# Token rows in order, inverted places and gathers between additions in a routed expert kernel

## What is computed

```python
x = x + _L1_ffn_ref(_layernorm(x), Wr, br, W1, b1, W2, b2)

def _L1_ffn_ref(x, Wr, br, W1, b1, W2, b2):      # E = 8 experts, D = 256, H = 1024
    scores = einsum('bsd,de->bse', x, Wr) + br
    _, topk_idx = top_k(scores, 2)
    indicator = one_hot(topk_idx, E).sum(-2)
    weights = softmax(where(indicator > 0, scores, -inf), axis=-1)
    for i in range(E):
        h = relu(x * indicator[..., i:i+1] @ W1[i] + b1[i])
        out = out + (h @ W2[i] + b2[i]) * weights[..., i:i+1]
    return out
```

## Time and profile before

| | |
|---|---|
| median of 3 runs | 1434.64 us |
| profiled execution, its own time | 1434.98 us |
| its span from first to last instruction | 1433.2 us |
| PE busy, share of the span | 1231.8 us, 86% |
| VectorE busy | 1025.3 us, 72% |
| ScalarE busy | 802.4 us, 56% |
| GpSimd busy | 522.3 us, 36% |
| mean granted clock of TensorE | 0.911 of 2.4 GHz |
| `route` block, about | 896 to 1007 us |
| `experts` block, about | 1007 to 1433 us |

### The profile page before, as it was taken

How to read it: one execution, slowest core, us unless ns; L and a number is a source line. 1 busy time by engine, 2 the same in 40 slices (tenths; PEclk the granted TensorE clock), 3 DMA queues, 4 the chain that set the end, 5 groups by cost and what they waited for, 6 DMA issues and landing times. The chain is left out here.

```text
span 1433.2 us, 28369 instructions
## 1 busy us (share of the span) xinstructions
PE 1231.8 (86%) x8633; PEld 930.1 (65%) x8634; DVE 1025.3 (72%) x2058; ACT 802.4 (56%) x1212; POOL 522.3 (36%) x423
## 2 busy tenths in 40 slices
PE   8959999976999594997999998741799999999995
PEld 4526777763433283784677676741689889998874
DVE  3759999877989686676788988766465665666543
ACT  2545665564679787636788876650333443344341
POOL 2027777720000000001887875576033223232322
PEclk9989999999999656999999999555899999999998
DMA  6020000000024675101132232565223232223210
GB/s 225 1 70 1 1 0 0 0 1 1 0 89 176 236 238 176 72 1 48 37 128 88 88 117 74 172 202 180 68 52 48 44 55 45 46 45 53 47 29 7
DMA packets 61447, 106.06 MB, mean 74 GB/s; under 512 B 7488, under 2 KB 48704, under 8 KB 60736
## 3 DMA queue, kind: packets, MB, share of 16 engines
q1 hardware_dynamic: 48080, 88.24, 19.2%
q0 software_dynamic: 13296, 16.92, 6.3%
HBM read 66.96 MB, written 39.10 MB: 74 GB/s over the span
## 5 line engine op out<-in xcount | busy, mean ns | idle before, releaser
L2308 POOL DMA_INDIRECT out<-ex_yo,ex_mt x71 | 115.4, 1625 | 314.4 <-DVE ex_yo L2283 170.9
L2217 ACT ACTIVATE ex_hT<-ex_ps_h,e_b1T,e_unscale 128x256 f32<-128x256 f32 (+1 forms) x312 | 143.9, 545 | 113.3 <-PE ex_ps_h L2174 113.3
L2174 PE MATMUL ex_ps_h<-ex_xT_hi,a_arena 128*128 128x256 f16 (+1 forms) x1248 | 203.5, 265 | 0.3 <-issue 0.2
L607 PE MATMUL at_ps_y<-c_VW,at_pT_hi 128*128 (+1 forms) x1024 | 171.1, 273 | 3.5 <-DVE main_x_res L740 3.5
L927 POOL TENSOR_TENSOR at_sc<-at_sc,at_ri 128x960 f32<-128x960 f32 (+1 forms) x96 | 145.2, 1527 | 68.7 <-DVE at_ri L735 68.0
L2174 PE MATMUL ex_ps_h<-ex_xT_lo,a_arena 128*128 128x256 f16 (+1 forms) x624 | 164.5, 264 | 0.0
L585 PE MATMUL at_ps_s<-a_arena,at_xnT_hi 128*128 (+1 forms) x512 | 158.8, 393 | 4.3 <-issue 4.3
L2187 PE MATMUL ex_ps_y<-a_arena,ex_hT_hi 128*128 x568 | 154.9, 273 | 4.7 <-DVE ex_hT_lo L2265 4.1
L2187 PE MATMUL ex_ps_y<-e_w_lo,ex_hT_hi 128*128 x568 | 154.9, 273 | 0.0
L2187 PE MATMUL ex_ps_y<-a_arena,ex_hT_lo 128*128 x568 | 154.8, 273 | 0.0
L927 POOL TENSOR_TENSOR at_sc<-at_sc,at_mx 128x960 f32<-128x960 f32 (+1 forms) x96 | 134.1, 1411 | 26.0 <-DVE at_mx L712 25.9
(11 more groups left out here) (350 smaller groups left out, 2811.0 us busy)
## 6 DMA issues: line engine op xcount, KB each, us to landing
at_half<-in_L_ffn_W SPq DMA_DIRECT2D x32, 512.0 KB, 4.0
up_scratch<-gm_stg SPq DMA_DIRECT2D x16, 768.0 KB, 3.2
gm_stg<-up_scratch SPq DMA_DIRECT2D x16, 768.0 KB, 4.3
ex_row<-xs SPq DMA_DIRECT2D x32, 260.0 KB, 3.0
rt_stage<-in_L_ffn_W SPq DMA_DIRECT2D x16, 512.0 KB, 5.4
main_x_res<-in_x SPq DMA_DIRECT2D x8, 512.0 KB, 12.1
out<-main_x_res SPq DMA_DIRECT2D x8, 512.0 KB, 6.3
xs<-rt_pad SPq DMA_DIRECT2D x18, 130.0 KB, 2.4
```

Of the source, the lines that this page charges most:

```text
L607: last = nc.tensor.matmul(ps_y[:, 0:D], a[j][:, n, :], b[:, bass.ds(off + n * D, D)], start=(n == 0 and i == 0), stop=(n == NP - 1 and i = ...
L2174: last = nc.tensor.matmul(ps_h[:, n, at], a[:, bass.ds(e * WN + d * HID + n * P, P)], b[:, d, at], start=(m == 0), stop=(m == 3 * DT - 1))
L2217: last = nc.scalar.activation(hT[:, n, at], ps_h[:, n, at], ACT.Relu, bias=b1T[:, bass.ds(e * HT + n, 1)], scale=unscale[:, 0, bass.ds(e, 1)])
L2308: nc.gpsimd.indirect_dma_start(out=acc[:, :], out_offset=bass.IndirectOffsetOnAxis(ap=mt[j][:, q, 1:2].bitcast(U32), axis=0), in_=yo[j][:, ...
```

## The change

In `route`, a token's row is sent once, in token order, by SP (one store for a group of four tiles). Positions are no longer computed per group: the one-hot vectors of all 32 tiles are kept, and after the last group VectorE computes for every token and both experts the place (slot and lane) that the row has in the experts' tiles. These places are inverted on PE: VectorE builds two 0/1 matrices per 16 token tiles and choice, GpSimd and ScalarE multiply one of them by the tile's number and by the lane's number, and 64 products sum them up, so that each lane of each of the 71 slots of 128 rows gets the number of its row in `xs`, in the table `slot`. Five small operations per group go from VectorE to GpSimd. In `experts`, a row tile is fetched by two indirect DMAs on GpSimd's queue, one for each slot, into one of four buffers; SP loads nothing there but a bias. Loops on PE, ScalarE and VectorE are unrolled by four instead of two, and GpSimd's is written out. The core of the diff:

```diff
@@ route, SP @@
-            sp.wait_ge(cnt_r, 1)
-            for e in range(E):
-                n = nc.sync.value_load(cnt[0:1, e:e + 1], min_val=0, max_val=T)
-                for q in range(TR // P):
-                    sp.dma_start(xs[bass.ds(n + (e * CAP + q * P), P), :], pad[:, :]).then_inc(padded, 16)
+            for c in range(NK):
+                sp.wait_ge(xn_r, TK * (c + 1))
+                sp.wait_ge(pay_r, c + 1)
+                sp.dma_start(xs[(TK * c + 1) * P:(TK * (c + 1) + 1) * P, :].rearrange("(i p) d -> p i d", p=P), pay[c % NB][:, :, :]
+                             ).then_inc(sent[c % NB], 16)
+                for q in range(NS + highs_to(c), min(NS + highs_to(c + 1), 2 * E)):
+                    load_half(q)
@@ route, GpSimd @@
-                for k in range(2):
-                    g.indirect_dma_start(out=xs[:, :], out_offset=bass.IndirectOffsetOnAxis(ap=pos[c % NB][:, i, k:k + 1], axis=0),
-                                         in_=pay[c % NB][:, i, :], in_offset=None, bounds_check=last_row,
-                                         oob_is_err=True).then_inc(sent[t % (NB * TK)], 16)
+                g.tensor_tensor(ind[:, mine, :], oh[:, 0, mine, :], oh[:, 1, mine, :], ALU.add).then_inc(ind_r, 1)
...
+            for n in range(NG):
+                pool.wait_ge(spot_r, n + 1)
+                need(pool, slot_mm, n - 1)
+                t0 = GR * n % NT
+                g.tensor_tensor(in_slot[n % 2][:, 0, :, :], is_slot[n % 2],
+                                turn_no[:, t0:t0 + GR].unsqueeze(2).to_broadcast([P, GR, SLOTS]), ALU.mult).then_inc(turn_r, 1)
@@ route, PE @@
+                for i in range(GR):
+                    last = nc.tensor.matmul(ps_i[:, 0:2 * SLOTS], in_lane[:, GR * g + i, :], in_slot[g % 2][:, :, i, :],
+                                            start=(g == 0 and i == 0), stop=(g == NG - 1 and i == GR - 1))
@@ route, VectorE: spread(g), four times @@
+                v.tensor_tensor(is_slot[g % 2], line[:, 0:SLOTS].unsqueeze(1).to_broadcast([P, GR, SLOTS]),
+                                part_f[:, 1, mine].unsqueeze(2).to_broadcast([P, GR, SLOTS]), ALU.is_equal).then_inc(spot_r, 1)
+                v.tensor_tensor(in_lane[:, mine, :], line[:, :].unsqueeze(1).to_broadcast([P, GR, P]),
+                                part_f[:, 0, mine].unsqueeze(2).to_broadcast([P, GR, P]), ALU.is_equal).then_inc(lane_r, 1)
@@ experts, SP @@
-                    sp.dma_start(row[j][:, q0:q1, :], xs[bass.ds(r * rows, rows), :].rearrange("(q p) d -> p q d", p=P)
-                                 ).then_inc(row_in[j], 16)
@@ experts, GpSimd @@
+            def fetch(i, q):
+                need(pool, t_r, i - RB + 1)
+                need(pool, meta_r, i - RB + 1)
+                n = 2 * i + q
+                nc.gpsimd.indirect_dma_start(out=row[i % RB][:, q, :], out_offset=None, in_=xs[:, :],
+                                             in_offset=bass.IndirectOffsetOnAxis(ap=slot[:, n:n + 1].bitcast(U32), axis=0),
+                                             bounds_check=last_sent, oob_is_err=True).then_inc(row_in[i % RB], 16)
+            for i in range(3):
+                for q in range(Q):
+                    fetch(i, q)
+            for k in range(NTL + 1):
+                for q in range(Q):
+                    if k and q < rows_of(k - 1).stop:
+                        add(k - 1, q)
+                    if there(k + 3, NTL) and q < rows_of(k + 3).stop:
+                        fetch(k + 3, q)
```

More of the change, by code:

```diff
@@ L1847, in _ @@
                     score(t - 1)
-                if t % TK == 2 and t > TK:
-                    rank(t // TK - 1)
             score(NT - 1)
-            rank(NK - 1)
+            rank()
+            for g in range(NG):
+                to_slots(g)
         @block.scalar
@@ L1891, in _ @@
             ratio(NK - 1)
+            for g in range(NG):
+                act.wait_ge(spot_r, g + 1)
+                need(act, slot_mm, g - 1)
+                nc.scalar.activation(in_slot[g % 2][:, 1, :, :], is_slot[g % 2], ACT.Copy, scale=lane[:, 0:1]).then_inc(slot_r, 1)
         @block.vector
@@ L1979, in place @@
             def place(c):
[L1981 to L1983 removed]
+                need(dve, pay_r, c)
                 dve.wait_ge(e_r, c + 1)
                 link_on(v.tensor_scalar(wt[:, 0, :], wt[:, 1, :], 1.0, None, ALU.add))
[L1986 to L1988 removed]
@@ L2006, in place @@
-                link_on(last)
-                for n in range(2):
-                    last = v.tensor_reduce(posf[:, :, n], oh[:, n, :, :], AX.X, ALU.add)
-                link_on(last)
-                v.tensor_copy(pos[c % NB][:, :, :], posf[:, :, :]).then_inc(meta_r, 1)
+                v.reciprocal(wt[:, 2, :], wt[:, 0, :]).then_inc(inv_r, 1)
             def lows(a, b):
@@ new lines, in _ @@
+            then(v.tensor_tensor(begin[:, 1, :], begin[:, 1, :], begin[:, 0, :], ALU.subtract))
+            then(v.tensor_tensor(incl[:, :, :], incl[:, :, :], begin[:, 1, :].unsqueeze(1).to_broadcast([P, NT, E]), ALU.mult))
+            then(v.tensor_tensor(after[:, :, :], after[:, :, :], incl[:, :, :], ALU.add))
+            for i in range(2):
+                last = v.tensor_tensor(oh[:, i, :, :], oh[:, i, :, :], after[:, :, :], ALU.mult)
+            then(last)
+            then(v.tensor_reduce(spot[:, :], oh[:, :, :, :].rearrange("p n t e -> p (n t) e"), AX.X, ALU.add))
@@ L2074, in experts @@
+            lows(highs_to(NK - 1), highs_to(NK))
+            dve.wait_ge(slot_mm, NG)
+            then(v.tensor_copy(lane_v[:, :], ps_i[:, SLOTS:2 * SLOTS]))
+            v.scalar_tensor_tensor(out=slot[:, :], in0=ps_i[:, 0:SLOTS], scalar=float(P), in1=lane_v[:, :],
+                                   op0=ALU.mult, op1=ALU.add)
+def experts(nc, b2, b1T, eid, x_res, w1, w2, unscale, ident, xs, acc, table, slot):
     Q = TR // P
     with Scope(nc, "ex") as s:
-        row = [s.sb(f"row{j}", [P, Q, ROW]) for j in range(2)]
+        RB = 4
+        row = [x_res[:, E:, :].rearrange("p t d -> p (t d)")[:, j * Q * ROW:(j + 1) * Q * ROW].rearrange("p (q d) -> p q d", q=Q)
+               for j in range(RB)]
@@ L2179, in down @@
             def down(i, j):
-                spans = [(look_up(nc.tensor, 1, n, E - 1), range(q0, q1)) for n, q0, q1 in runs(i)]
+                spans = [(expert(nc.tensor, n), range(q0, q1)) for n, q0, q1 in runs(i)]
                 pe.wait_ge(hlo_r, 2 * i + 2)
@@ L2210, in relu @@
             def relu(i, j):
[L2211 removed]
+                spans = [(expert(nc.scalar, n), slice(q0 * P, q1 * P)) for n, q0, q1 in runs(i)]
                 for g in range(2):
```

279 lines of the change are left out of this document (143 added, 136 removed).

## The result

The changed kernel takes 1541.22 us (median of 4 runs, 1538.81 to 1544.16), the kernel before 1426.16 us (4 runs, 1415.17 to 1437.44): a ratio of 1.0836, 95% interval 1.0733 to 1.0938. The profiled execution took 1544.16 us, its span 1542.0. By their times two of the four runs of before have this long start (1434.64 and 1437.44 us) and none of the changed kernel's, so the ratio is a little low: against 1417.6 us, the median of the 13 runs of before taken beside e1, it is 1.087.

The account below looks back on a forecast made before the run. PE was taken to bound the expert loop and no engine to be full in routing; 1434.98 + 114 (30 steps, 3.80 us wait each) - 5 (routing) = 1544 us, range 1485 to 1605.

Parts of the forecast that it names:

- The chain of a step: Expert loop: from one step's start through yo, additions and second gather to PE's next start, 14.72 us against 10.92.
- The estimate of 2.3 us: Expert loop: alternative time for a 133 KB gather to land, in place of 3.0; total 21 us lower.
- The mixed steps cover it: Expert loop after the 30 lengthened steps: mixed steps already take 15.12 us, so the 14.72 us chain adds nothing.
- The clock rival: Expert loop: waits let TensorE's clock fall, opening transposition +0.5 us per step, 15 us, 1559 in all; chance 0.13.
- the share of three quarters for PE: Expert loop, a sign: PE's busy share falls to about three quarters, from 50.00 of 50 us.
- The routing: Before the expert loop: 17 us gained in the group loop, 11.8 lost computing places after it, a gain of 5 us.
- the term for `spread`: Routing, after the last one-hot: four times `spread` on VectorE, 14.5 us, with the multiplications and PE's products running under it.
- the 2.1 us per group in the loop: Routing loop: each of 8 groups falls from 8.56 to 6.5 us, 17 us earlier at the last one-hot.
- The 243 GB/s: Routing loop: transfer rate taken to limit each group, 1.58 MB in 6.5 us.
- The low end of the forecast's range: Whole kernel: 1485 us, from a chain of 13.0 us and -12 for the routing.
- First transposition and last one-hot: End of routing, signs: last one-hot near 967 us, first expert transposition near 1005 us.
- The sign that was to show the forecast wrong: End of routing: the prediction is wrong if the first expert transposition is later than 1015 us.

Follow-up runs that it names:

- e1: Changed kernel with both gathers ahead of both additions in each turn of GpSimd's loop: 1422.31 us, ratio to the kernel before 1.0041.
- e4: Changed kernel with eight row buffers instead of four and gathers for tile k+4 instead of k+3, still alternating with the additions: 1424.67 us.
- e5: On top of e1, GpSimd's multiplication under `spread` made by ScalarE, as 16 small operations per group: 1414.08 us.
- e7: On top of e1, the five small routing operations per group moved from GpSimd back to VectorE: 1433.82 us, in an execution with the long start.
- e0: The kernel before, unchanged, run once more with a profile: 1419.83 us.

## Why the prediction came out, step by step

- **The chain of a step: right, term by term.** Forecast 4.88 to the first addition, 5.0, 1.84, 3.0, 14.72; measured 4.78, 4.71, 2.08, 3.30, 14.88. From the last gather's start to PE's, which no row of before had, it was 2.9 us at the median of the 21 steps in which that gather's issue took 1.06 us or little more, and 3.7 on the mean of the nine in which it took 1.8. The loss in 30 steps was 118 us against 114. That the place in the queue is the cause, and not slower transfers, e1 to e4 show. The estimate of 2.3 us from the Trainium skill's page on DMA ("DMA: Bandwidth & Descriptors", "Anatomy of one DMA — SWDGE (gpsimd) path") would have been 0.6 too low against that 2.9, and 1.0 against the mean of 3.30.
- **The mixed steps cover it: nearly.** The rest behind tile 33 grew by 4.6 us where nothing was forecast. The first mixed stretch ran at a granted clock of 0.89, that of e1 at 1.00 (1347.4 to 1361.9), and e1's rest is 74.2 us long.
- **The clock rival: right that it falls, wrong in its price.** With waits of 2 to 4 us ahead of each step the granted clock was 0.93 over the 30 steps, where it was 1.00: in 15 stretches, 58 us in all, it stood at 0.50. But the rival's 0.5 us per step was paid in 7 of the 31 steps alone, whose opening transposition took 1.07 to 1.12 us and whose `yo` ended 4.20 after the step's start instead of 3.79; that is 0.1 us per step, and the first addition stands 4.78 after the start, no later than forecast. The rest of what PE loses comes out of its wait, which was 2.4 us per step and not the 3.80 of the forecast or the 3 to 5 named as a sign. So the share of three quarters for PE is off too: 41.77 of 50, 84%.
- **The routing: wrong in sign.** Forecast a gain of 5 us; measured a loss of 5.6 (113.7 to 119.3). The first step that failed is the term for `spread`. Its comparisons alone were sized well (4 x 3.45 = 13.8 in e5, forecast 14.5), and 16-bit operands with a broadcast did run at the slow rate, 1.33 us per 1136 columns, as the Trainium skill's page "VectorE: DVE Perf Modes", section "What auto-detection actually checks", has it, which the prediction weighed. But "GpSimd's and ScalarE's multiplications and PE's 64 products run under it" is false for GpSimd: its 1.94 us per group add to VectorE's, 19.5 us up to the line behind, and that line waits out the last one (2.42 for 0.54). All that stands behind the last one-hot takes 44.4 us where 38.2 were forecast. The second is the 2.1 us per group in the loop: from the first one-hot to the last the gain is 78.6 - 66.3 = 12.3 us, not 17. That "five small operations per group go to GpSimd, which has only those to do there" left out that they stand in front of the row store and of the half loads behind it; without them on GpSimd the loop gives 7.0 us more (e7). The 243 GB/s did not set the loop: in e7 the same bytes move in 7.0 us less.
- **The total: closer than its parts, by luck.** 1544 against 1541.2, but the routing missed by 10.6 us, loop and rest by 8.4 more, and the 19.6 us by which the two profiled executions differ ahead of the routing, 17.7 of them in the start, made up for it. From e0's 1419.83 the same terms give 1529, 15 us under the 1544.16 of the profiled execution. Against e0, with the usual start, the change costs 1542.0 - 1418.1 = 123.9 us of span. The order in GpSimd's loop is 120.4 of it (to e1's 1421.6) and the routing 5.7 (113.6 to 119.3); the 2.2 us by which the two exceed the sum lie within the 3.1 that e0 took more behind its first transposition. The low end of the forecast's range takes off 12 us for the routing where its own bound of a gain is 11; nothing hangs on that.
- **First transposition and last one-hot.** Named for 1005 and 967, found at 995.8 and 951.4. Counted from the first half load they are at 119.3 and 74.9, where the forecast's are 108.9 and 70.9: both late, not early. The sign that was to show the forecast wrong, a first transposition later than 1015, is 118.9 when counted so, and by 0.4 us it was there: for the routing, as above.

## What to carry to other kernels

A prefetch is as early as its place in the queue that issues it: count, for each transfer, what stands ahead of it there and which step that belongs to; the four buffers of this kernel did not help while the list put it behind this step's last result, and one reordered line (e1) was worth 119 us. Work handed to GpSimd is off VectorE's path only if the two do not read SBUF at the same time in the way seen here (two inputs on VectorE's side), and only if nobody waits for its result; a 0.2 us operation that must wait out a 1.2 us one, with a store and the next loads behind it, cost 7 us. Compare two traces by the lengths of their stages, counted from a point behind the last stage that the change leaves alone, before any difference of absolute times is believed.

## What the runs showed of the hardware

- A VectorE operation on two SBUF tensors and a GpSimd operation exclude each other over whole instructions: VectorE's 1.34 us becomes 3.22, GpSimd's 0.20 becomes 1.15, and with ScalarE in GpSimd's place all four comparisons take 1.33 or 1.34 (e5).
- A gather of 128 rows of 1040 bytes takes GpSimd 1.06 us to issue in most steps; of the eight in turn ahead of the loop (991.06 to 1000.64) seven take 1.01, 1.32 from start to start. It lands 2.8 us after its start at the least, 3.0 at the median. Some issues take 1.8 us; beside each of those in the changed kernel's 30 steps VectorE's second splitting operation on the ReLU's result (line 2297) ran, which was not tried apart.
- The same fp32 products in the first stage took 0.43 or 0.71 us by the execution, 18 us in all: where they took 0.71, the clock's record begins only behind them, at 50.94 us and not at some 11, and until then TensorE ran at its lower level. Why it rises later is open.
- With waits of 1.7 to 3.8 us ahead of steps of some 15 us the granted clock was 0.93 where it was 1.00 without waits; the transposition that opens a step was slow in 7 steps of 31.
